# Causal attention with a routed expert layer: joined diagonal key tiles, written-out groups, and side matmuls behind a step's values

## The chip, the cores and the metric

The kernel runs on one core of one Trainium2 chip. The metric is the device time of one execution in microseconds, from the first to the last instruction and what lies around it. Three runs of the kernel before gave 377.74, 378.73 and 380.70 us; the median is 378.73.

## The reference

x has 2048 tokens of 128 features. It is normalised, and two branches are added to it: causal attention with 16 heads of 8 features, and a layer of 8 experts in which each expert takes the 512 tokens with the highest router probability.

```python
xn = _layernorm(x, axis=-1)
# attention, per head
att = jnp.einsum('bhqd,bhkd->bhqk', q, k) * scale
att = jnp.where(causal, att, -jnp.inf)
y = jnp.einsum('bhqk,bhkd->bhqd', softmax(att), v)
# experts
probs = softmax(jnp.einsum('bsd,ed->bse', xn, choice_w))
G, I = jax.lax.top_k(jnp.swapaxes(probs, -1, -2), k)      # k = 512
h = jax.nn.silu(jnp.einsum('bekd,edf->bekf', x_in, w1))    # x_in = xn[I]
x_mlp = jnp.einsum('bekf,efd->bekd', h, w2)
out = x + projected_attention + zeros.at[b_idx, I].add(G[..., None] * x_mlp)
```

## The kernel before, in words

**Tiling.** The heads are done in 4 groups (G) of 4 heads (HG), one group behind the other. In a group the 2048 queries are cut into 4 chunks of 512 (N), and the keys into 16 tiles of 128 (P). A step k is one pair of a query chunk c and a key tile j; causality leaves 4, 8, 12 and 16 steps for the four chunks, 40 in all (NS). The last four steps of a chunk are its diagonal tiles: their key tile lies 0, 128, 256 and 384 queries into the chunk, so they are 512, 384, 256 and 128 queries wide (`off` cuts the rest away) and have one 128 x 128 block that is to be masked.

**A step.** It has two units u = 2k and 2k + 1, one for each pair of heads. For a unit TensorE makes the scores of two heads (`score`, L1146) into one of three double banks of PSUM, ScalarE takes the exponential of both (L691) into `probs`, which has four buffers, one per step. For diagonal steps VectorE masks the block with a minimum (`mask`, L998), once for each unit. Then TensorE multiplies the values with the probabilities of all four heads (`values`, L1163), accumulating over the steps of a chunk in `acc`. The value matmul has float32 operands and is recorded as eight matmuls, 32 output rows for each head. Sums of probabilities come with it, from a column of ones in `v_grp`. At a chunk's end VectorE copies `acc` (L1014), and the next chunk's first values wait for that copy.

**Side work.** Beside the attention steps, groups 0 to 3 do a piece of the router or of an expert in each of some steps, a "turn": group 0 the search for each expert's threshold by bisection (`search`, 30 rounds: TensorE sums comparisons over tokens, L1171; VectorE reduces and makes the next candidate, L890 to L897), group 1 the lists of chosen tokens (`route`, one-hot tiles on VectorE, L941, packed by TensorE, L1196), groups 2 and 3 four experts each (`expert`). An expert has seven turns, one per full-width step: transposing the gathered tokens (L1216), two turns with half of w1 each (L1224), two turns in which only VectorE works (L979), two with half of w2 each (L1232), after which VectorE scales by the gate (`y_exp`, L986) and GpSimd scatters the rows with an added store to DRAM (L600). The hidden halves are copied from PSUM by VectorE (L974), and ScalarE takes their tanh (L680), behind the first exponential of the step two later. All turns share one bank, `spare`.

**Order of the work.** Each engine has its own queue, written by hand and worked through in order; engines meet at semaphores. TensorE's order in step k is: the scores of unit 2k + 3, the turn, the scores of unit 2k + 4, the values of step k. Scores of unit u wait for the exponential of unit u - 3. VectorE's order in groups 0 and 1 is: the copy of `acc` at a chunk's end, the turn of step k, the mask of step k + 1; in groups 2 and 3 the mask comes ahead of the turn. The four lines that matter:

```python
# VectorE, group(): groups 0 and 1 have turn_first=True
if k in turns and turn_first:
    turn(turns.index(k))
if k + 1 < NS:
    mask(g, k + 1)
# TensorE, values(): the first wait of a diagonal step
pe.wait_ge(s_mask, 2 * NT * g + 2 * MASKED.index(k) + 2)
# TensorE, search(): the turn waits for VectorE, and VectorE's next for it
pe.wait_ge(s_above, k)
```

Groups 0 and 1 are written out on TensorE and VectorE, groups 2 and 3 are a loop of two rounds there; ScalarE has two loops of two, and the queue of transfers (SP), which brings the next group's queries and keys, a loop of three and one group written out. The functions that the diff touches:

## Time and profile before

| what | value |
|---|---|
| median of three runs | 378.73 us |
| the profiled execution | 376.79 us |
| its span | 374.7 us |
| around the span | 2.1 us |
| TensorE busy (matmuls) | 326.4 us |
| ScalarE busy | 295.5 us |
| VectorE busy | 218.5 us |
| GpSimd busy | 126.5 us |
| mean granted TensorE clock | 0.954 |

PE is TensorE, PEld its weight loads, DVE VectorE, ACT ScalarE, POOL GpSimd, SP the queue that issues most transfers. Busy times are unions over overlapping instructions, and instructions of one engine can overlap: an exponential of 128 x 1024 is recorded with a duration longer than the distance to the next one's start. From start to start is therefore the measure of a pace, and the duration that of a latency. The group starts can be told by the copies to `v_grp` (L1007, from 51.3 to 280.2 us).

### The profile page before, as it was taken

How to read it: one execution, taken by the hardware profiler on the slowest of the kernel's cores; microseconds unless marked ns; L12 is line 12 of the kernel's file. 1: busy time of each engine (PE TensorE's matmuls, PEld its weight loads, DVE VectorE, ACT ScalarE, POOL GpSimd, SP SyncE). 2: the span in 40 equal slices, each digit the busy share in tenths (PEclk: the TensorE clock that was granted, in tenths of full speed). 3: DMA queues.
4: the chain of work that ended last, by engine and by line, in shares of the span. 5: the costliest groups of instructions: out<-in, count | busy, mean ns of one | idle time of the engine just before them, and what ended most of it. 6: DMA issues, size and time to landing. Idle time of an engine off the chain costs nothing.

```text
span 374.7 us, 7404 instructions
## 1 busy us (share of the span) xinstructions
PE 326.4 (87%) x2453; PEld 109.5 (29%) x2453; DVE 218.5 (58%) x606; ACT 295.5 (79%) x376; POOL 126.5 (34%) x122
## 2 busy tenths in 40 slices
PE   0774848899999699999998989999999899999972
PEld 0442702122222122222222232424242233232362
DVE  4849987866766888669657353342255432526443
ACT  1297729589899688988997989899979899898800
POOL 8420243800000000038830008584868041606150
PEclk9999559699999999999999999999999999999996
DMA  6044575710110210014422113151436131312057
GB/s 169 0 167 117 159 274 209 210 52 0 52 46 22 71 52 24 29 30 132 117 65 71 53 33 52 53 107 52 83 88 128 42 73 14 49 39 21 7 89 224
DMA packets 33679, 30.69 MB, mean 82 GB/s; under 512 B 3688, under 2 KB 28480, under 8 KB 33648
## 3 DMA queue, kind: packets, MB, share of 16 engines
q1 hardware_dynamic: 27248, 24.00, 19.9%
q0 software_dynamic: 6400, 6.30, 10.4%
q8 instruction: 17, 0.28, 0.3%
q14 instruction: 14, 0.11, 0.1%
HBM read 14.36 MB, written 15.93 MB: 81 GB/s over the span
## 4 chain that ended last, share of the span: by engine, by line
PE 69%; DVE 16%; ACT 5%; issue 4%; DMA 4%; POOL 1%; POOLq 1%; DVEq 0%; SPq 0%; ACTq 0%
PE bank L1163 31%; PE bank L1146 20%; PE bank L1232 5%; PE bank L1224 5%; DVE probs L998 4%; ACT probs L691 3%; PE bank L1196 2%; DVE onehot L941 2%; PE bank L1110 2%; DMA x_sb<-in_L_attn_x_dram 1%; DVE cand L895 1%; DMA xn<-total_dram 1%; DMA total_dram<-m_space,token 1%; PE bank L1171 1%; PE bank L1074 1%
## 5 line engine op out<-in xcount | busy, mean ns | idle before, releaser
L691 ACT ACTIVATE probs<-bank 128x1024 f32<-128x1024 f32 (+3 forms) x320 | 264.0, 934 | 41.2 <-PE bank L1146 39.2
L1163 PE MATMUL bank<-probs,v_grp 128*32 128x512 f32 (+3 forms) x1280 | 153.7, 553 | 12.5 <-DVE probs L998 11.8
L1146 PE MATMUL bank<-q_aug,k_aug 51*128 51x512 bf16 (+3 forms) x640 | 106.8, 358 | 3.2 <-ACT probs L691 2.9
L600 POOL DMA_INDIRECT total_dram<-m_space,token x32 | 50.4, 1575 | 93.7 <-DVE m_space L986 86.4
L998 DVE TENSOR_TENSOR probs<-probs,causal 128x256 f32<-128x256 f32 x128 | 50.6, 425 | 37.8 <-ACT probs L691 37.1
L1146 PEld LDWEIGHTS bank<-q_aug,k_aug 51*128 51x128 bf16 x640 | 27.6, 93 | 149.4 <-ACT probs L691 109.7
L941 DVE TENSOR_SCALAR onehot<-slot_iota,slot 128x512 bf16<-128x512 f16 x128 | 37.0, 357 | 9.7 <-PE bank L1196 9.7
L1163 PEld LDWEIGHTS bank<-probs,v_grp 128*32 128x32 f32 x1280 | 25.4, 108 | 51.2 <-DVE probs L998 19.1
L577 POOL DMA_DIRECT2D w_x<-in_L_ffn_w_dram x8 | 7.5, 943 | 90.7 <-DVE gate L960 90.7
L580 POOL DMA_INDIRECT parts<-xn_dram,token x32 | 31.8, 992 | 9.7 <-issue 9.7
L974 DVE COPY m_space<-bank 128x512 f32<-128x512 f32 x16 | 11.0, 687 | 24.2 <-PE bank L1224 24.2
L1232 PE MATMUL bank<-w_x,hT 128*128 128x128 f32 x128 | 18.5, 288 | 2.6 <-DVE hT L979 2.6
L1014 DVE COPY y_acc<-bank 128x512 f32<-128x512 f32 x16 | 11.1, 691 | 14.2 <-PE bank L1163 14.2
L1224 PE MATMUL bank<-xgT,w_x 128*128 128x512 f32 x32 | 18.0, 645 | 0.0
L1232 PEld LDWEIGHTS bank<-w_x,hT 128*128 128x128 f32 x128 | 15.5, 191 | 6.1 <-issue 3.1
L890 DVE TENSOR_REDUCE passed<-bank 128x8 f32<-128x128 f32 x30 | 8.7, 289 | 14.6 <-PE bank L1171 14.6
L1196 PE MATMUL bank<-onehot,parts 128*32 128x512 bf16 x128 | 12.8, 389 | 1.9 <-DVE onehot L941 1.9
L986 DVE TENSOR_TENSOR m_space<-bank,gate 128x512 f32<-128x512 f32 x8 | 5.5, 690 | 13.4 <-PE bank L1232 13.4
L979 DVE SCALAR_TENSOR_TENSOR hT<-th,m_space 128x512 f32<-128x512 f32 x16 | 11.0, 685 | 4.1 <-ACT th L680 4.1
L680 ACT ACTIVATE th<-m_space 128x512 f32<-128x512 f32 x16 | 10.3, 642 | 0.0
L1074 PE MATMUL bank<-xnT,wT 128*128 128x512 f32 x16 | 9.5, 722 | 0.8 <-ACT xnT L617 0.8
L897 DVE TENSOR_TENSOR above<-r_p,cand 128x128 bf16<-128x128 f32 x30 | 8.9, 296 | 1.0
(128 smaller groups left out, 237.7 us busy)
## 6 DMA issues: line engine op xcount, KB each, us to landing
y_dram<-y_acc SPq DMA_DIRECT2D x16, 256.0 KB, 2.2
q_aug<-product_dram SPq DMA_DIRECT2D x32, 96.0 KB
k_aug<-product_dram SPq DMA_DIRECT2D x32, 96.0 KB, 2.4
w_x<-in_L_ffn_w_dram POOLq DMA_DIRECT2D x16, 128.0 KB, 2.8
product_dram<-parts SPq DMA_DIRECT2D x4, 384.0 KB, 3.2
product_dram<-parts SPq DMA_DIRECT2D x6, 256.0 KB, 3.0
product_dram<-parts SPq DMA_DIRECT2D x2, 768.0 KB, 4.8
x_sb<-in_L_attn_x_dram SPq DMA_DIRECT2D x4, 256.0 KB, 4.7
```

The costliest lines, as they stand in the source:

```text
L580: pool.indirect_dma_start(x_got[:, i, t, :], None, xn_dram, bass.IndirectOffsetOnAxis(ap=token[:, e, t:t + 1], axis=0))\
L600: pool.indirect_dma_start(total_dram, bass.IndirectOffsetOnAxis(ap=token[:, e, t:t + 1], axis=0), y_exp[:, e % 2, t, :], None, compute_op= ...
L691: act.activation(probs[:, (u // 2) % PB, 2 * p:2 * p + 2, off:N], scores[u % SB][:, :, off:N], ACT.Exp, scale=SCALE).then_inc(s_exp, 1)
L941: last = dve.tensor_scalar(onehot[:, i % 2, a, :], slot_iota[:, :], slot[:, n, e:e + 1], None, ALU.is_equal)
L998: dve.tensor_tensor(tile, tile, causal[:, :].unsqueeze(1).broadcast_to([P, 2, P]), ALU.min).then_inc(s_mask, 1)
L1014: dve.tensor_copy(y_acc[:, c % 2, :], acc).then_inc(s_accfree, 1)
L1074: pe.matmul(flat(f + i), wT[:, i, :], xnT[:, c * N:(c + 1) * N], start=True, stop=True)
L1146: last = pe.matmul(scores[u % SB][:, a, off:N], k_aug[HEAD_ROWS[a], p, j * P:(j + 1) * P], q_aug[HEAD_ROWS[a], p, c * N + off:(c + 1) * N] ...
L1163: last = pe.matmul(acc[32 * h:32 * h + 32, off:N], v_grp[:, j, h, :], probs[:, k % PB, h, off:N], start=(k in CHUNK_START), stop=(k in CHU ...
L1196: last = pe.matmul(spare[PK_W * a:PK_W * (a + 1), :], payload[:, n, EPP * s + a, :], onehot[:, i % 2, a, :], start=(n == 0), stop=(n == NT ...
L1224: pe.matmul(spare, w1_x[:, i, f * P:(f + 1) * P], xgT[:, :], start=True, stop=True)\
L1232: last = pe.matmul(spare[:, t * C:(t + 1) * C], hT[:, f, t * P:(t + 1) * P], w2_x[:, i, f, :], start=(f == 0), stop=(f == FH - 1))
```

## The change

**Steps and units.** A chunk's four diagonal steps become three. The first is the full-width tile as before. The second holds two tiles, the one of 384 and the one of 128 queries, side by side in the 512 columns of a unit; its mask covers two blocks (the first and the last 128 columns). The third holds the tile of 256 queries and has one unit, for all four heads, 4 x 256 columns. So every unit has 1024 columns; there are 36 steps and 68 units in a group instead of 40 and 80. The third kind of step takes no search turn; experts' turns stand in steps of full width alone, the router's in every step. The banks of PSUM go on turning over from one group to the next, and the first units of a group wait, like all others, for the exponential three units before (the function `before` goes).

**Order on TensorE.** In each step first the scores of the units ahead, together (`scores_ahead`), then the step's values, then the turn.

**Loops.** All groups are written out on all engines, with constants where registers were.

```diff
@@ -47,14 +47,30 @@
     HALF = P // 2
 
 
-    STEPS = [(c, j) for c in range(NC) for j in range(TPC * (c + 1))]
...
+    STEPS = []
+    for _c in range(NC):
+        _d = TPC * _c
+        STEPS += [(_c, [(j, 0, N, 0)], []) for j in range(_d)]
+        STEPS += [(_c, [(_d, 0, N, 0)], [0]),
+                  (_c, [(_d + 1, P, N - P, 0), (_d + 3, N - P, P, N - P)], [0, N - P]),
+                  (_c, [(_d + 2, 2 * P, 2 * P, 0)], [0])]
     NS = len(STEPS)
...
+    HALF_STEP = [k for k in range(NS) if STEPS[k][1][0][2] == N // 2]
+    CHUNK_END = [max(k for k in range(NS) if STEPS[k][0] == c) for c in range(NC)]
...
-    MASKED = [k for k in range(NS) if STEPS[k][1] >= TPC * STEPS[k][0]]
-
-    FIRST_OF_KEYS = [min(k for k in MASKED if STEPS[k][0] == c) for c in range(NC)]
-    NU = 2 * NS
+    FIRST_OF_KEYS = [CHUNK_END[c] - 2 for c in range(NC)]
+
+
+    UNITS = [(k, p) for k in range(NS) for p in ([(0, 1)] if k in HALF_STEP else [(0,), (1,)])]
+    NU = len(UNITS)
+    FIRST_UNIT = [min(u for u in range(NU) if UNITS[u][0] == k) for k in range(NS)]
+    LAST_UNIT = [max(u for u in range(NU) if UNITS[u][0] == k) for k in range(NS)]
+
+    MASKS = [sum(len(UNITS[u:v]) for u, v in
+                 [(FIRST_UNIT[i], LAST_UNIT[i] + 1) for i in range(k + 1) if STEPS[i][2]]) for k in range(NS)]
     SB = 3
...
-    SEARCH_STEPS = [k for k in range(NS) if WIDTH[k] > N // 2]
-    EXPERT_STEPS = [k for k in range(NS) if WIDTH[k] == N]
-    ROUTE_STEPS = [k for k in range(NS) if WIDTH[k] > P]
+    SEARCH_STEPS = [k for k in range(NS) if k not in HALF_STEP]
+    EXPERT_STEPS = [k for k in range(NS) if k not in HALF_STEP and k + 1 not in HALF_STEP]
+    ROUTE_STEPS = list(range(NS))
...
-            with sp.Fori(0, G - 1) as g:
-                group(g, False)
-            group(G - 1, True)
+            for g in range(G):
+                group(g, g == G - 1)
...
+            def expert_tanh(g, i):
                 if i % TPE in H_TURN:
-                    e, f = EPG * x + i // TPE, H_TURN.index(i % TPE)
...
+            def exponentials(g, u):
+                k, pairs = UNITS[u]
+                buf = scores[(NU * g + u) % SB]
+                own = probs[:, (NS * g + k) % PB]
+                act.wait_ge(s_sready, NU * g + u + 1)
+                if u == FIRST_UNIT[k]:
+
+                    act.wait_ge(s_pfree, NS * g + k + 1)
+                if k in HALF_STEP:
+                    src = buf[:, :, :].rearrange("q a (p n) -> q a p n", p=2)
+                    dst = own[:, :, 0:N // 2].rearrange("q (p a) n -> q a p n", a=2)
+                else:
+                    src, dst = buf[:, :, :], own[:, 2 * pairs[0]:2 * pairs[0] + 2, :]
+                act.activation(dst, src, ACT.Exp, scale=SCALE).then_inc(s_exp, 1)
+
+            for g in range(G):
                 for u in range(NU):
-                    c, j = STEPS[u // 2]
-                    off = max(0, j - TPC * c) * P
-                    p = u % 2
-                    act.wait_ge(s_sready, NU * g + u + 1)
-                    if p == 0:
-
-                        act.wait_ge(s_pfree, NS * g + u // 2 + 1)
-                    act.activation(probs[:, (u // 2) % PB, 2 * p:2 * p + 2, off:N],
-                                   scores[u % SB][:, :, off:N], ACT.Exp, scale=SCALE).then_inc(s_exp, 1)
-                    if extra and p == 0 and u // 2 - 2 in EXPERT_STEPS:
-                        extra(EXPERT_STEPS.index(u // 2 - 2))
-
-            with act.Fori(0, EXPERT_G) as g:
-                group(g)
-            with act.Fori(0, G - EXPERT_G) as x:
-
-                group(x + EXPERT_G, lambda i: expert_tanh(x, i))
+                    exponentials(g, u)
+                    k = UNITS[u][0]
+                    if g >= EXPERT_G and u == FIRST_UNIT[k] and k - 2 in EXPERT_STEPS:
+                        expert_tanh(g, EXPERT_STEPS.index(k - 2))
 
...
             def mask(g, k):
-                c, j = STEPS[k]
-                if k in MASKED:
-                    off = (j - TPC * c) * P
-                    for p in range(2):
-
-                        dve.wait_ge(s_exp, NU * g + SB + 2 * k + p + 1)
-                        tile = probs[:, k % PB, 2 * p:2 * p + 2, off:off + P]
-                        dve.tensor_tensor(tile, tile, causal[:, :].unsqueeze(1).broadcast_to([P, 2, P]),
-                                          ALU.min).then_inc(s_mask, 1)
+                places = STEPS[k][2]
+                if not places:
+                    return
+                own = probs[:, (NS * g + k) % PB].rearrange("q h (b n) -> q h b n", n=P)
+                own = own[:, :, 0:TPC:TPC - 1, :] if len(places) == 2 else own[:, :, 0:1, :]
+                for u in range(FIRST_UNIT[k], LAST_UNIT[k] + 1):
+                    pairs = UNITS[u][1]
+                    tile = own[:, 2 * pairs[0]:2 * pairs[-1] + 2]
+                    dve.wait_ge(s_exp, NU * g + SB + u + 1)
+                    dve.tensor_tensor(tile, tile, causal[:, :].unsqueeze(1).unsqueeze(1).broadcast_to(
+                        [P, 2 * len(pairs), len(places), P]), ALU.min).then_inc(s_mask, 1)
...
-                for k, (c, j) in enumerate(STEPS):
+                for k in range(NS):
+                    c = STEPS[k][0]
                     if k in CHUNK_END:
 
...
             group(THRESHOLD_G, SEARCH_STEPS, search, turn_first=True)
             group(ROUTE_G, ROUTE_STEPS, route, turn_first=True)
-            with dve.Fori(0, G - EXPERT_G) as x:
-                group(x + EXPERT_G, EXPERT_STEPS, lambda i: expert(x, i))
+            for g in range(EXPERT_G, G):
+                group(g, EXPERT_STEPS, lambda i: expert(g - EXPERT_G, i))
 
...
             def score(g, u):
-                k, p = u // 2, u % 2
-                c, j = STEPS[k]
-                off = max(0, j - TPC * c) * P
-                if p == 0 and k in CHUNK_START:
+                k, pairs = UNITS[u]
+                c, blocks, _ = STEPS[k]
+                if u == FIRST_UNIT[k] and k in CHUNK_START:
                     pe.wait_ge(s_stage_q[c], 16 * 4 * (g + 1))
-                if p == 0 and k in FIRST_OF_KEYS:
+                if u == FIRST_UNIT[k] and k in FIRST_OF_KEYS:
                     pe.wait_ge(s_stage_k[c], 16 * 2 * (g + 1))
 
-                pe.wait_ge(s_exp, NU * g + SB + before(u))
-                for a in range(2):
-                    last = pe.matmul(scores[u % SB][:, a, off:N],
-                                     k_aug[HEAD_ROWS[a], p, j * P:(j + 1) * P],
-                                     q_aug[HEAD_ROWS[a], p, c * N + off:(c + 1) * N], start=True, stop=True)
+                pe.wait_ge(s_exp, NU * g + u + 1)
+                for i, p in enumerate(pairs):
+                    for j, first, width, at in blocks:
+                        at += i * (N // 2)
+                        for a in range(2):
+                            last = pe.matmul(scores[(NU * g + u) % SB][:, a, at:at + width],
+                                             k_aug[HEAD_ROWS[a], p, j * P:(j + 1) * P],
+                                             q_aug[HEAD_ROWS[a], p, c * N + first:c * N + first + width],
+                                             start=True, stop=True)
                 last.then_inc(s_sready, 1)
 
             def values(g, k):
-                c, j = STEPS[k]
-                off = max(0, j - TPC * c) * P
+                c, blocks, places = STEPS[k]
                 if k == 0:
                     pe.wait_ge(s_vgrp, g + 1)
                 if k in CHUNK_START:
                     pe.wait_ge(s_accfree, NC * g + c + 1)
-                if k in MASKED:
-                    pe.wait_ge(s_mask, 2 * NT * g + 2 * MASKED.index(k) + 2)
+                if places:
+                    pe.wait_ge(s_mask, MASKS[-1] * g + MASKS[k])
                 else:
-                    pe.wait_ge(s_exp, NU * g + SB + 2 * k + 2)
-                for h in range(HG):
-                    last = pe.matmul(acc[32 * h:32 * h + 32, off:N], v_grp[:, j, h, :], probs[:, k % PB, h, off:N],
-                                     start=(k in CHUNK_START), stop=(k in CHUNK_END))
+                    pe.wait_ge(s_exp, NU * g + SB + LAST_UNIT[k] + 1)
+                for j, first, width, at in blocks:
+                    for h in range(HG):
+                        last = pe.matmul(acc[32 * h:32 * h + 32, first:first + width], v_grp[:, j, h, :],
+                                         probs[:, (NS * g + k) % PB, h, at:at + width],
+                                         start=(k in CHUNK_START), stop=(k in CHUNK_END))
                 last.then_inc(s_pfree, 1)
...
+            def scores_ahead(g, k):
+
+                for u in range(FIRST_UNIT[k] + LEAD, LAST_UNIT[k] + LEAD + 1):
+                    if u < NU:
+                        score(g, u)
+                    elif g + 1 < G:
+                        score(g + 1, u - NU)
+
             def group(g, turns, turn):
                 for k in range(NS):
-                    if 2 * k + LEAD < NU:
-                        score(g, 2 * k + LEAD)
+                    scores_ahead(g, k)
+                    values(g, k)
                     if k in turns:
                         turn(turns.index(k))
-                    if 2 * k + LEAD + 1 < NU:
-                        score(g, 2 * k + LEAD + 1)
-                    if k == NS - 1:
-                        next_group(g)
-                    values(g, k)
-
-            def next_group(g):
-
-                if isinstance(g, int):
-                    for u in range(LEAD):
-                        score(g + 1, u)
-                else:
-                    with pe.If(g < G - 1):
-                        for u in range(LEAD):
-                            score(g + 1, u)
 
             for u in range(LEAD):
                 score(0, u)
             group(THRESHOLD_G, SEARCH_STEPS, search)
             group(ROUTE_G, ROUTE_STEPS, route)
-            with pe.Fori(0, G - EXPERT_G) as x:
-                group(x + EXPERT_G, EXPERT_STEPS, lambda i: expert(x, i))
+            for g in range(EXPERT_G, G):
+                group(g, EXPERT_STEPS, lambda i: expert(g - EXPERT_G, i))
 
...
```

On TensorE, first group, from the last unmasked step of chunk 2 into its diagonal (bank: PSUM; q_aug, k_aug: scores; v_grp: values; above: the search's comparisons). Before:

```order
L1163 MATMUL bank<-probs,v_grp 32x512 [waits probs_ready]
L1163 MATMUL bank<-probs,v_grp 32x512 x3
L1146 MATMUL bank<-q_aug,k_aug 128x384 [waits probs_ready]
L1146 MATMUL bank<-q_aug,k_aug 128x384
L1171 MATMUL bank<-above,ones_pp 128x128 [waits candidates_compared]
L1146 MATMUL bank<-q_aug,k_aug 128x256 [waits probs_ready]
L1146 MATMUL bank<-q_aug,k_aug 128x256
L1163 MATMUL bank<-probs,v_grp 32x512 [waits causal_masked]
L1163 MATMUL bank<-probs,v_grp 32x512 x3
```

After:

```order
L1178 MATMUL bank<-probs,v_grp 32x512 [waits probs_ready]
L1178 MATMUL bank<-probs,v_grp 32x512 x3
L1187 MATMUL bank<-above,ones_pp 128x128 [waits candidates_compared]
L1160 MATMUL bank<-q_aug,k_aug 128x384 [waits probs_ready]
L1160 MATMUL bank<-q_aug,k_aug 128x384
L1160 MATMUL bank<-q_aug,k_aug 128x128 x2
L1160 MATMUL bank<-q_aug,k_aug 128x256 [waits probs_ready]
L1160 MATMUL bank<-q_aug,k_aug 128x256 x3
L1178 MATMUL bank<-probs,v_grp 32x512 [waits causal_masked]
L1178 MATMUL bank<-probs,v_grp 32x512 x3
L1187 MATMUL bank<-above,ones_pp 128x128 [waits candidates_compared]
```

The search's matmul of the masked step stood two places ahead of that step's values (the L1171 in the middle) and now stands behind them; the two units' scores stand together.

On VectorE, same place: passed, cand, thr and above are the search's turn, probs the mask, y_acc the copy of the sum. Before, from the chunk's last turn:

```order
L890 TENSOR_REDUCE passed<-bank 128x8 [waits tokens_above_counted]
L891 SCALAR_TENSOR_TENSOR cand<-passed,cand 128x8 [waits threshold_step]
L893 TENSOR_TENSOR thr<-thr,cand 128x8 [waits threshold_step]
L895 TENSOR_SCALAR cand<-thr 128x8 [waits threshold_step]
L897 TENSOR_TENSOR above<-r_p,cand 128x128 [waits threshold_step]
L998 TENSOR_TENSOR probs<-probs,causal 128x2x128 [waits probs_ready] x4
L1014 COPY y_acc<-bank 128x512 [waits y_sent1,probs_used]
```

After:

```order
L900 TENSOR_REDUCE passed<-bank 128x8 [waits tokens_above_counted]
L901 SCALAR_TENSOR_TENSOR cand<-passed,cand 128x8 [waits threshold_step]
L903 TENSOR_TENSOR thr<-thr,cand 128x8 [waits threshold_step]
L905 TENSOR_SCALAR cand<-thr 128x8 [waits threshold_step]
L907 TENSOR_TENSOR above<-r_p,cand 128x128 [waits threshold_step]
L1010 TENSOR_TENSOR probs<-probs,causal 128x4x128 [waits probs_ready]
L1027 COPY y_acc<-bank 128x512 [waits y_sent1,probs_used]
```

Turn and mask keep their order; four masks of two blocks are now one of four.

On TensorE, third group, a step of the first expert with half of w1 (xgT, w_x). Before:

```order
L1146 MATMUL bank<-q_aug,k_aug 128x512 [waits probs_ready]
L1146 MATMUL bank<-q_aug,k_aug 128x512
L1223 ISA
L1224 MATMUL bank<-xgT,w_x 128x512 [waits hidden_copied]
L1144 REGISTER_ALU
L1146 MATMUL bank<-q_aug,k_aug 128x512 [waits probs_ready]
L1146 MATMUL bank<-q_aug,k_aug 128x512
L1163 MATMUL bank<-probs,v_grp 32x512 [waits probs_ready]
L1163 MATMUL bank<-probs,v_grp 32x512 x3
```

After:

```order
L1160 MATMUL bank<-q_aug,k_aug 128x512 [waits probs_ready]
L1160 MATMUL bank<-q_aug,k_aug 128x512
L1160 MATMUL bank<-q_aug,k_aug 128x512 [waits probs_ready]
L1160 MATMUL bank<-q_aug,k_aug 128x512
L1178 MATMUL bank<-probs,v_grp 32x512 [waits probs_ready]
L1178 MATMUL bank<-probs,v_grp 32x512 x3
L1240 MATMUL bank<-xgT,w_x 128x512 [waits hidden_copied]
```

The w1 matmul has moved from between the two units' scores to behind the step's values.

## Rows read from the trace of the kernel before

**Rows 1.** Page, part 1: busy us (share of the span) and instructions.
```profile
PE 326.4 (87%) x2453; PEld 109.5 (29%) x2453; DVE 218.5 (58%) x606; ACT 295.5 (79%) x376; POOL 126.5 (34%) x122
```

**Rows 2.** Busy time by stretch (us; PE, PEld, DVE, ACT, POOL, granted clock, DMA, GB/s).
```profile
67.10:73.90 6.80, 6.43 (x34) 1.03 (x26) 5.91 (x17) 2.91 (x5) 6.21 (x10) 0.50 0.85 252
...
203.40:281.40 78.00, 75.83 (x576) 24.54 (x576) 31.55 (x61) 69.78 (x89) 38.78 (x33) 1.00 0.31 67
```

**Rows 3.** Timeline, first group, full step (start, us, engine, line, out<-in, count).
```profile
81.60 1.06 PE L1163 MATMUL bank<-probs,v_grp 128*32 128x512 f32 x8
...
82.60 0.39 PE L1146 MATMUL bank<-q_aug,k_aug 51*128 51x512 bf16 x2
...
82.92 0.23 PE L1171 MATMUL bank<-above,ones_pp 128*128 128x128 bf16 x1
...
83.44 1.06 PE L1163 MATMUL bank<-probs,v_grp 128*32 128x512 f32 x8
```

**Rows 4.** Timeline, ScalarE, same stretch.
```profile
79.27 10.21 ACT L691 ACTIVATE probs<-bank 128x1024 f32<-128x1024 f32 x11
```

**Rows 5.** Groups by shape: busy us, mean ns | idle before, releaser.
```profile
L691 ACT ACTIVATE probs<-bank 128x1024 f32<-128x1024 f32 x224 | 212.2, 1068 | 11.8 <-PE bank L1146 11.2
...
L998 DVE TENSOR_TENSOR probs<-probs,causal 128x256 f32<-128x256 f32 x128 | 50.6, 425 | 37.8 <-ACT probs L691 37.1
...
L691 ACT ACTIVATE probs<-bank 128x256 f32<-128x256 f32 x32 | 12.2, 382 | 8.3 <-PE bank L1146 7.5
...
L680 ACT ACTIVATE th<-m_space 128x512 f32<-128x512 f32 x16 | 10.3, 642 | 0.0
...
L986 DVE TENSOR_TENSOR m_space<-bank,gate 128x512 f32<-128x512 f32 x8 | 5.5, 690 | 13.4 <-PE bank L1232 13.4
```

**Rows 6.** Timeline, first group, into the diagonal of chunk 3.
```profile
118.50 0.23 PE L1171 MATMUL bank<-above,ones_pp 128*128 128x128 bf16 x1
...
118.77 0.29 DVE L890 TENSOR_REDUCE passed<-bank 128x8 f32<-128x128 f32 x1 [0.70 <-PE bank L1171]
...
119.91 0.93 DVE L998 TENSOR_TENSOR probs<-probs,causal 128x256 f32<-128x256 f32 x2
...
120.89 0.64 PE L1163 MATMUL bank<-probs,v_grp 128*32 128x512 f32 x4 [0.17 <-DVE probs L998]
```

**Rows 7.** Timeline, TensorE, first group, diagonal of chunk 2.
```profile
90.78 1.06 PE L1163 MATMUL bank<-probs,v_grp 128*32 128x512 f32 x8
...
97.46 0.42 PE L1163 MATMUL bank<-probs,v_grp 128*32 128x128 f32 x8
...
98.75 0.64 PE L1163 MATMUL bank<-probs,v_grp 128*32 128x512 f32 x4
```

**Rows 8.** Timeline, third group, expert steps.
```profile
261.74 1.06 PE L1163 MATMUL bank<-probs,v_grp 128*32 128x512 f32 x8
...
263.06 1.13 PE L1224 MATMUL bank<-xgT,w_x 128*128 128x512 f32 x2
...
264.22 0.69 DVE L974 COPY m_space<-bank 128x512 f32<-128x512 f32 x1 [2.00 <-PE bank L1224]
...
264.44 1.06 PE L1163 MATMUL bank<-probs,v_grp 128*32 128x512 f32 x8
...
268.67 1.07 PE L1163 MATMUL bank<-probs,v_grp 128*32 128x512 f32 x8
...
270.20 1.06 PE L1163 MATMUL bank<-probs,v_grp 128*32 128x512 f32 x8
```

**Rows 9.** Waits: engine, line <- releaser: us in total, times, longest us.
```profile
PE bank L1232 <- DVE hT L979: 2.6, 2, 1.3
```

**Rows 10.** Timeline, fourth group, last diagonal.
```profile
352.19 1.16 PE L1232 MATMUL bank<-w_x,hT 128*128 128x128 f32 x8
...
353.50 1.06 PE L1163 MATMUL bank<-probs,v_grp 128*32 128x512 f32 x8
353.50 0.69 DVE L986 TENSOR_TENSOR m_space<-bank,gate 128x512 f32<-128x512 f32 x1
```

25 lines of the change are left out of this document (9 added, 16 removed).

## Prediction

> **What bounds the kernel now.** I read the page first, then the busy time by stretch, then the timeline step by step. TensorE is busy for 87% of the span and ScalarE for 79% [rows 1], an average over four head groups that do different side work. By stretch: the third group, which carries experts, has TensorE busy 75.83 of 78.00 us and ScalarE 69.78 [rows 2]. So in the expert groups nearly every microsecond that TensorE is given or spared counts, and ScalarE has some 8 us of air in a group.
>
> I call V(k) the eight value matmuls of step k, S a unit's scores, T(k) the side matmul of a step (search, router, expert). In the first group the V at 81.60 is followed by S 82.60, T 82.92, another S, and V 83.44: 1.84 us a step [rows 3]. Its pieces, from start to start, are V 1.00, S 0.32, T 0.20, S 0.32: TensorE works without a break. ScalarE's exponentials in that stretch, eleven in 10.21 us, the last one about 1.07 long by the group's mean, start (10.21 - 1.07) / 10 = 0.91 us apart [rows 4, 5]: 1.82 a step. The two engines are almost level there, and neither can catch up quickly.
>
> **The diagonal units.** Exponential instructions go from 320 (224 of 1024 elements and three shorter forms of 32 each) to 272, 48 fewer, masks from 128 [rows 5] to 80, most of them of twice the size. TensorE's columns are the same (384 + 128 instead of two steps, 256 for four heads instead of two units), so where TensorE is the bound the packing gives only a few tile switches. An exponential of 1024 elements takes 1.07 and one of 256 takes 0.38 [rows 5]: 0.69 for 768 elements, 0.92 per 1024, which leaves 0.15 fixed in an instruction, but the start spacing of 0.91 shows that most of that overlaps with the next one. I value the 48 instructions at nothing on the path and hide them behind TensorE; the ends are -2.4 us (48 x 0.05, were ScalarE the bound) and 0. The Trainium skill, "ScalarE: Activation LUTs", section "What ACT_TABLE_LOAD costs", gives an activation 186 ns plus 0.833 ns per element; by it 48 fewer would spare 8.9 us and the sum would come out 8.9 lower. The rows agree with that as the length of one, not as the distance of two.
>
> **What the new order does in the first group.** The order on VectorE does not change: turn(k) of the search (L890 to L897) waits for T(k), and mask(k+1) stands behind it. Before, T(k) stands ahead of V(k), so that chain runs beside a whole V. The last diagonal shows how tight that is: T at 118.50, reduce 118.77, above 119.69, masks 119.91 for 0.93, V at 120.89 [rows 6], 2.39 us from T to the V of the next step, of which TensorE already idles 0.17. After, T(k) stands behind V(k). Then V(k+1) <- mask(k+1) <- turn(k) <- T(k) <- V(k) is one serial loop, at each masked step. Its links: V 1.00, then 2.39 from T to V. For the joined step b each mask has 512 elements, which costs 0.69 as the other VectorE operation of that size on 128 partitions does [rows 5] against 0.42, so 2 x 0.27 = 0.54 more: 2.93. For the half step c one such mask: 2.39 - 0.93 + 0.69 = 2.15, with waits say 2.3. V takes 1.06 for 512 columns [rows 3] and 0.42 for 128 [rows 7], so 0.21 for each 128, and start to start 0.15 more: V of b, in two pieces, is 1.14, V of c 0.57. From the short last V to the next chunk's V it is 1.29 now (97.46 to 98.75 [rows 7]: the accumulator's copy), so 1.50 with 0.21 more columns. A chunk's end, from V(a-1) to the next chunk's first V, is then (1.00 + 2.39) + (1.00 + 2.93) + (1.14 + 2.3) + 1.50 = 12.3 us. Now it is 98.75 - 90.78 = 7.97 [rows 7]. That is +4.3 for three loops, 1.43 each. Chunk 0 has one loop (the first turn needs no matmul), chunks 1 and 2 have three, chunk 3 two (behind the joined step the search marks its result and waits for no T): nine loops, 12.9 us. The 21 full steps gain from one S beside the other (two in a row take 0.54, not 0.64: a step without T is 1.53 [rows 8], less 1.00 for V) until ScalarE's 1.82 stops them: -0.5. **First group +12.4.** ScalarE's lead of three units does not absorb this: it keeps ScalarE busy, but V is late, and afterwards TensorE needs 1.73 and ScalarE 1.82 a step, so nothing is made good.
>
> **TensorE's clock.** The granted clock was 0.50 (1.2 GHz) for the 6.80 us from 67.10 [rows 2], at the diagonal of chunk 1, where the search waits for VectorE already. The new diagonals leave TensorE idle about half the time. Not falling again costs 0; 1.2 GHz through the diagonals of chunks 2 and 3 and a step or two behind each costs up to 7 (seven or eight V at up to 1.0 each). I take one more fall as long as the one shown, two V: +2.0. The Trainium skill, "TensorE: Matmul & The Clock Gate", section "HAM oscillation — how this bites in real kernels", warns of just such a kernel that waits between bursts; by it the sum would be nearer +7.
>
> **Router group.** Its T of 512 bf16 columns is taken like an S, 0.32; the step is then 0.32 + 0.32 + 0.32 + 1.00 = 1.96 now, 1.86 after, about 24 times: -2.4. The turn makes one-hots for the next T, so there is no loop in ordinary masked steps; two joined masks are a little cheaper than three or four, -0.5 in all. Four turns do need their own step's T and have a mask or a copy behind them (ranks, the first list, the last copy, the last list); each comes a V later: +4.0. **+1.1**, ends -2.9 and +5.
>
> **Expert groups.** A step with T is 264.44 - 261.74 = 2.70 now [rows 8], 2.60 after; one without is 270.20 - 268.67 = 1.53 in both. 20 steps with T in a group: -2.0. One stall goes: TensorE waits 2 x 1.3 us for hT (L979) [rows 9], at the diagonal of chunk 1; after, V covers it: -1.3. A new one comes: ScalarE runs tanh for step k behind the first exponential of step k+2. That exponential's scores now come before V(k) and T(k), not behind T(k). Now T at 263.06 leads to the copy at 264.22 (0.69) [rows 8], 1.16 later, and none of the 16 tanh waited [rows 5]. After, with V(k) at 0: T 1.00, copy 2.16 to 2.85, while the exponential started at about 0.9 and ScalarE is free at 1.8: tanh waits 1.1 us, and the next one 0.3 more. Followed on, the next exponentials start at 3.4 and 4.3, the second tanh at 5.5, the exponential behind it at 6.0, done at 7.0. TensorE, with V at 0, 2.60, 5.20 and 6.74, asks for that one at 6.5, before the V of the second step without T, and gets it at 7.1; there the pair of S is split as well, so V comes at 7.4, 0.7 late, and a step on another 0.25 late: 0.95 in all. Four experts in a group: +3.8. Four accumulator waits with the wider last V: +0.8. **+1.3 in the third group, +1.1 up to the last diagonal of the fourth.** Ends: -3.3 without any tanh effect, +4.
>
> **The end.** The last expert's product (T at 352.19, y_exp at 353.50 [rows 10]) starts POOL's scatters, which lead to the end. It now stands ahead of the diagonal's V (353.50); behind it, it ends 1.00 + 1.16 later instead of level: **+2.2**. The written-out loops change no order inside a group. No row prices a loop's turn by itself; TensorE's idle time in the looped third group, 78.00 - 75.83 = 2.2 us [rows 2], bounds the gain, and as much the loss from more code to load. I put it at 0, since that idle time has other causes named above.
>
> **Sum.** 12.4 + 2.0 + 1.1 + 1.3 + 1.1 + 2.2 = 20.1 us on the profiled execution's 376.8: 396.9, say 397. That execution is 1.9 below the median of 378.7 and within the runs' 3.0 spread, so I add nothing.
>
> **Rivals.**
> A, faster: the loop through VectorE never decides, since exponentials and tile switches carry the time. Place: diagonals of the first group. Price: the chunk's end shrinks to TensorE's own work of about 6.7 instead of 7.97, -3.9 in three chunks; with -0.5, -2.9, twice -3.3, and the end's +2.2 it is 365 us. It decides if T to V takes less than the 0.73 that T and two S give as cover; 2.39 speaks against it. 0.08.
> B, expert groups gain: tanh finds its operand because TensorE's lead over ScalarE is smaller than I assume. Then twice the 3.8 go, 397 - 7.6 = 389.4, and with a third off the first group's term 385. For it: ScalarE is now idle in steps with T. 0.20.
> C, the clock stays at half in the first group's diagonals and on into full steps, and the router's late turns meet it: +5 to +8, 402 to 405. 0.17.
> D, halfway: the loop costs half of 12.4 and the expert groups gain as in A, 397 - 6.2 - 7.6 - 2.0 (no fall of the clock) = 381, near the edge of no change. 0.05.
> The forecast: 0.50.
>
> **How the numbers follow.** About 1% is what a measurement of this kernel can tell from no change. Faster 0.08 is A; the same 0.05 is D; slower 0.87 is the forecast with B and C. The range runs from B's low end to just past C's: 385 to 406, with A and D outside and a little above.
>
> **What would show it.** In the profile after, the first group's V starts at the diagonals should be about 3.4, 3.9 and 3.4 us apart and VectorE's reduce should come 0.27 behind a T that follows V; the expert groups should last 79 us with tanh rows that sat idle behind VectorE's copy; y_exp of the last expert should start 2 us after the last 512-wide masked V. I am wrong if chunk 2 of the first group ends in under 9 us, if tanh shows no wait, or if exponentials start under 0.91 apart in full steps.

## The result, and the profile after

Slower, as forecast. Five runs of the changed kernel have a median of 396.06 us (393.26 to 396.56), five of the kernel before in the same session 379.82: a ratio of 1.043, 95% interval 1.038 to 1.047. The forecast was 397. The profiled execution took 393.26 with a span of 391.5, 16.8 more than before; both profiled executions are at the fast end of their kernel's runs, 2.8 and 3.0 under these medians.

The page after: busy time, the slices of TensorE and the granted clock.

```profile
PE 320.4 (82%) x2453; PEld 107.8 (28%) x2453; DVE 214.9 (55%) x558; ACT 290.1 (74%) x328; POOL 128.1 (33%) x122
...
PE   1775856589599749997997899999998999999971
...
PEclk9997558969779998998999999999999999999995
```

TensorE is busy for 6 us less and the span is 17 us longer [rows 1]: the loss is waiting. Each digit is a fortieth of the span, 9.8 us: the low ones in the 6th to the 14th (first group) and a few in the 15th to the 22nd (router) show where. The groups' starts, read from the first V of each:

| stretch | before | after | difference | forecast |
|---|---|---|---|---|
| up to the first V | 52.6 | 53.5 | +0.9 | 0 |
| first group (search) | 75.8 | 88.1 | +12.3 | +12.4 and +2.0 of clock |
| second group (router) | 75.0 | 76.3 | +1.2 | +1.1 |
| third group (experts) | 78.1 | 78.8 | +0.7 | +1.3 |
| fourth, to its last diagonal | 72.1 | 72.5 | +0.4 | +1.1 |
| end | 21.2 | 22.4 | +1.2 | +2.2 |

Every group's time holds the luck of the clock as well. In the first group TensorE's granted clock was at half for 11.1 us before and for 25.3 after (over the group it is 0.93 and 0.86). The kernel of e6 below has the first group's order of the kernel before, but its clock was at half there for 22.3 us, and the group took 80.4 instead of 75.8. That is 0.42 us for each further microsecond at half clock. Other pairs of profiles with one order give 0.17 (e10 against the changed kernel, first group: 89.4 against 88.1, 32.8 at half against 25.3) and 0.45 (e1 against it, third group: 80.1 against 78.8, 2.9 against 0). So a difference of a microsecond between two single profiles shows nothing before the clock has been compared.

The waits after, in total, times and longest (us). The first row was 11.8, 15 times, before; the second 14.6, 23 times; the third had no counterpart.

```profile
PE bank L1178 <- DVE probs L1010: 33.6, 20, 5.4
DVE passed L900 <- PE bank L1187: 29.5, 30, 3.4
ACT th L688 <- DVE m_space L984: 8.9, 8, 1.5
```

The timeline after, first group, diagonal of chunk 2 (L1178: V, L1187: T, L1160: S, L900 to L907: the search's turn, L1010: masks, L1027: copy of acc). It answers to [rows 6, 7].

```profile
96.02 1.06 PE L1178 MATMUL bank<-probs,v_grp 128*32 128x512 f32 x8
...
97.01 0.23 PE L1187 MATMUL bank<-above,ones_pp 128*128 128x128 bf16 x1
...
97.28 0.29 DVE L900 TENSOR_REDUCE passed<-bank 128x8 f32<-128x128 f32 x1 [0.52 <-PE bank L1187]
...
98.42 0.76 DVE L1010 TENSOR_TENSOR probs<-probs,causal 128x256 f32<-128x256 f32 x2
...
99.23 1.06 PE L1178 MATMUL bank<-probs,v_grp 128*32 128x512 f32 x8 [1.31 <-DVE probs L1010]
...
100.23 0.23 PE L1187 MATMUL bank<-above,ones_pp 128*128 128x128 bf16 x1
...
102.98 1.93 PE L1178 MATMUL bank<-probs,v_grp 128*32 128x384 f32 x16 [1.98 <-DVE probs L1010]
...
104.85 0.29 PE L1187 MATMUL bank<-above,ones_pp 128*128 128x128 bf16 x1
...
107.05 1.08 PE L1178 MATMUL bank<-probs,v_grp 128*32 128x256 f32 x8 [1.38 <-DVE probs L1010]
...
109.03 1.93 PE L1178 MATMUL bank<-probs,v_grp 128*32 128x512 f32 x8
```

Here the loop can be read link by link: V 96.02, T 97.01, reduce 97.28, masks 98.42, V 99.23, and again. The V are 3.21, 3.75, 4.07 and 1.98 apart, 13.0 us where it was 7.97 before; forecast 12.3. In the full steps ahead of that diagonal, on the other hand, TensorE runs at 1.70 a step:

```profile
89.08 1.07 PE L1178 MATMUL bank<-probs,v_grp 128*32 128x512 f32 x8
...
90.78 1.06 PE L1178 MATMUL bank<-probs,v_grp 128*32 128x512 f32 x8
```

The timeline after, third group, the first expert's two steps with w1 (L1240) and the two free steps behind them; it answers to [rows 8].

```profile
225.32 1.07 PE L1178 MATMUL bank<-probs,v_grp 128*32 128x512 f32 x8
225.62 0.63 ACT L688 ACTIVATE th<-m_space 128x512 f32<-128x512 f32 x1 [1.08 <-DVE m_space L984]
...
226.32 1.12 PE L1240 MATMUL bank<-xgT,w_x 128*128 128x512 f32 x2
...
227.91 1.07 PE L1178 MATMUL bank<-probs,v_grp 128*32 128x512 f32 x8
...
230.13 1.07 PE L1178 MATMUL bank<-probs,v_grp 128*32 128x512 f32 x8
...
232.09 1.07 PE L1178 MATMUL bank<-probs,v_grp 128*32 128x512 f32 x8
```

The step with T takes 2.59, as forecast, the first tanh idles 1.08 (forecast 1.1), and the two free steps take 2.22 and 1.96 where they were 1.53 each.

### The profile page after: what moved, and what is told of

Its sections match the earlier page's. It is cut to its first block, busy times and chain, and to the rows that moved or that the text cites. A ratio compares the mean times of both kernels' runs of the same rounds, so it can differ in the third digit from the quotient of the medians.

```text
span 391.5 us, 6404 instructions
## 1 busy us (share of the span) xinstructions
PE 320.4 (82%) x2453; PEld 107.8 (28%) x2453; DVE 214.9 (55%) x558; ACT 290.1 (74%) x328; POOL 128.1 (33%) x122
## 4 chain that ended last, share of the span: by engine, by line
PE 59%; DVE 22%; ACT 9%; issue 5%; DMA 3%; POOL 1%; POOLq 0%; SPq 0%; DVEq 0%; ACTq 0%
PE bank L1178 30%; PE bank L1160 12%; ACT probs L703 6%; DVE probs L1010 5%; PE bank L1248 4%; PE bank L1240 4%; DVE y_acc L1027 2%; PE bank L1122 2%; PE bank L1212 1%; DVE m_space L984 1%; PE bank L1187 1%; DVE onehot L951 1%; PE bank L1232 1%; DMA xn<-total_dram 1%; DVE cand L905 1%
## 5 line engine op out<-in xcount | busy, mean ns | idle before, releaser
L703 ACT ACTIVATE probs<-bank 128x1024 f32<-128x1024 f32 x272 | 256.4, 1060 | 50.8 <-PE bank L1160 49.9
L1178 PE MATMUL bank<-probs,v_grp 128*32 128x512 f32 (+3 forms) x1280 | 155.4, 569 | 36.0 <-DVE probs L1010 33.6
L1160 PE MATMUL bank<-q_aug,k_aug 51*128 51x512 bf16 (+3 forms) x640 | 92.8, 366 | 6.1 <-ACT probs L703 5.5
L608 POOL DMA_INDIRECT total_dram<-m_space,token x32 | 51.4, 1606 | 95.8 <-DVE m_space L996 88.5
L1010 DVE TENSOR_TENSOR probs<-probs,causal 128x512 f32<-128x512 f32 (+1 forms) x80 | 44.8, 580 | 26.5 <-ACT probs L703 26.2
L1178 PEld LDWEIGHTS bank<-probs,v_grp 128*32 128x32 f32 x1280 | 28.0, 112 | 96.9 <-issue 39.2
L1160 PEld LDWEIGHTS bank<-q_aug,k_aug 51*128 51x128 bf16 x640 | 22.2, 95 | 76.1 <-ACT probs L703 50.8
L951 DVE TENSOR_SCALAR onehot<-slot_iota,slot 128x512 bf16<-128x512 f16 x128 | 37.8, 362 | 7.3 <-PE bank L1212 7.0
L900 DVE TENSOR_REDUCE passed<-bank 128x8 f32<-128x128 f32 x30 | 8.7, 292 | 29.5 <-PE bank L1187 29.5
L1027 DVE COPY y_acc<-bank 128x512 f32<-128x512 f32 x16 | 11.1, 692 | 19.0 <-PE bank L1178 19.0
L1240 PE MATMUL bank<-xgT,w_x 128*128 128x512 f32 x32 | 18.0, 645 | 0.0
L1187 PEld LDWEIGHTS bank<-above,ones_pp 128*128 128x128 bf16 x30 | 2.9, 97 | 28.4 <-DVE above L907 18.8
```

Source lines behind the costliest of these rows:

```text
L608: pool.indirect_dma_start(total_dram, bass.IndirectOffsetOnAxis(ap=token[:, e, t:t + 1], axis=0), y_exp[:, e % 2, t, :], None, compute_op= ...
L703: act.activation(dst, src, ACT.Exp, scale=SCALE).then_inc(s_exp, 1)
L951: last = dve.tensor_scalar(onehot[:, i % 2, a, :], slot_iota[:, :], slot[:, n, e:e + 1], None, ALU.is_equal)
L1010: dve.tensor_tensor(tile, tile, causal[:, :].unsqueeze(1).unsqueeze(1).broadcast_to([P, 2 * len(pairs), len(places), P]), ALU.min).then_in ...
L1027: dve.tensor_copy(y_acc[:, c % 2, :], acc).then_inc(s_accfree, 1)
L1160: last = pe.matmul(scores[(NU * g + u) % SB][:, a, at:at + width], k_aug[HEAD_ROWS[a], p, j * P:(j + 1) * P], q_aug[HEAD_ROWS[a], p, c * N ...
```

## The experiments

All but e4 and e6 start from the changed kernel; e4 and e6 start from the one before. Each was timed in three rounds beside the kernel before (medians 378.8 to 379.9). All compute the whole reference. The code is cut to the lines that matter. "g1 72.5" means that the first group took 72.5 us in the profiled execution.

### e1_search_early: the old order, in the first group alone

```diff
- scores_ahead(g, k)
+ early = g == THRESHOLD_G
+ scores_ahead(g, k, slice(0, 1))
+ if early and k in turns:
+     turn(turns.index(k))
+ scores_ahead(g, k, slice(1, None))
  values(g, k)
- if k in turns:
+ if not early and k in turns:
      turn(turns.index(k))
```

The slice picks which of the step's units get their scores.

> The changed kernel, with TensorE's order of the kernel before (scores, turn, scores, values) in the first group alone. Theory L (a serial loop values, search matmul, VectorE's turn, mask, next values): the first group falls from 88 us to between 73 and 76, the diagonal of its chunk 2 from 13.0 us to under 8, the granted clock there stays 1.00, and the profiled execution comes to about 380 (393 less 13). Rival P (the joined and half steps with their larger masks cost it, the order is harmless): no change, 391 to 395. Rival U (the written-out loops cost it): no change.

Measured: 378.36 us, ratio 1.000 (0.997 to 1.003); g1 72.5, g2 76.1, g3 80.1. The profile of e1 at the same diagonal:

```profile
90.14 1.06 PE L1178 MATMUL bank<-probs,v_grp 128*32 128x512 f32 x8
...
91.46 0.23 PE L1187 MATMUL bank<-above,ones_pp 128*128 128x128 bf16 x1
...
91.94 1.07 PE L1178 MATMUL bank<-probs,v_grp 128*32 128x512 f32 x8
...
94.21 1.07 PE L1178 MATMUL bank<-probs,v_grp 128*32 128x384 f32 x16 [0.40 <-DVE probs L1010]
...
95.95 0.64 PE L1178 MATMUL bank<-probs,v_grp 128*32 128x256 f32 x8 [0.34 <-DVE probs L1010]
...
97.41 1.06 PE L1178 MATMUL bank<-probs,v_grp 128*32 128x512 f32 x8
```

V to V this chunk's end takes 7.27 instead of 13.0: T stands ahead of V, so the search's turn runs beside it. The place of one small matmul in one group is worth 17.7 us in the medians (396.06 - 378.36) and 15.0 in the profiled spans, about as much as the whole change costs (16.2 and 16.8). That sum holds the clock too: in the first group it was at half for 11.6 us here and for 25.3 in the changed kernel.

### e2_masks_first: TensorE untouched, masks ahead of the turn on VectorE

```diff
- group(THRESHOLD_G, SEARCH_STEPS, search, turn_first=True)
+ group(THRESHOLD_G, SEARCH_STEPS, search)
```

> The changed kernel, with the mask of step k+1 ahead of the search's turn k on VectorE in the first group, as groups 3 and 4 have it. TensorE's order is untouched, so the search matmul still stands behind the values. L: the mask no longer waits for that matmul, the loop is open, and the first group falls to 74 to 77 us, the whole to about 381. P and U: no change, 391 to 395. Were it the place on TensorE as such (its matmul late, whoever waits), also no change.

Measured: 379.62, ratio 1.000 (0.998 to 1.002); g1 74.5. Here TensorE's order is that of the changed kernel, word for word, and the loss is gone all the same. So what costs is the loop V, T, turn, mask, V, and it can be cut at either of the two edges tried. TensorE's order by itself costs the first group little: g1 is 2.0 above e1's 72.5 and 1.3 below the 75.8 of the kernel before.

### e3_tanh_late: tanh behind the step's second exponential

```diff
- if g >= EXPERT_G and u == FIRST_UNIT[k] and k - 2 in EXPERT_STEPS:
+ if g >= EXPERT_G and u == LAST_UNIT[k] and k - 2 in EXPERT_STEPS:
```

> The changed kernel, with ScalarE's tanh for step k behind the second exponential of step k+2, not the first. L: the 8 waits of tanh (8.9 us in all) go, the gap between the V of the two steps without a side matmul falls from 2.21 and 1.92 to about 1.6 and 1.8, and the two expert groups lose 2 to 4 us each: 386 to 389. Rival: the waits lie in ScalarE's slack and nothing moves, 392 to 394.

Measured: 391.2, ratio 1.032 (1.028 to 1.037), less gain than expected; in the profile the third group takes 77.2 against 78.8, 0.4 per expert, not 0.95, and from the fourth group's start to the end it is 92.9 against 94.9, 0.5 per expert. No tanh waits any more, but ScalarE's wait for scores in the third group grows. The waits of ScalarE in that group, of the changed kernel (217.8 to 296.6 us):

```profile
ACT probs L703 <- PE bank L1160: 5.5, 10, 1.6
ACT th L688 <- DVE m_space L984: 4.3, 4, 1.1
```

of e3 (218.8 to 296.0):

```profile
ACT probs L703 <- PE bank L1160: 8.3, 15, 1.6
```

and of e11_best_orders below (196.1 to 272.3), with the old order in the expert groups:

```profile
ACT probs L703 <- PE bank L1160: 7.0, 19, 1.0
```

The timeline of e3, TensorE, the same expert's free steps:

```profile
228.95 1.07 PE L1178 MATMUL bank<-probs,v_grp 128*32 128x512 f32 x8
...
230.49 1.06 PE L1178 MATMUL bank<-probs,v_grp 128*32 128x512 f32 x8
...
232.27 0.39 PE L1160 MATMUL bank<-q_aug,k_aug 51*128 51x256 bf16 x4 [0.39 <-ACT probs L703]
...
232.73 1.06 PE L1178 MATMUL bank<-probs,v_grp 128*32 128x512 f32 x8
```

The first free step has shrunk from 2.22 to 1.54, but the second has grown from 1.96 to 2.24, with TensorE waiting for an exponential. 4.3 us of waits for tanh's operand are gone and 2.8 of waits for scores have come. ScalarE waits 9.8, 8.3 and 7.0 us in the group in these three kernels, and the group takes 78.8, 77.2 and 76.2. But its work is the same in all three, so time less waits has to come out equal (69.0, 68.9, 69.2) and doesn't say which engine sets the pace; TensorE is idle 4.8, 3.9 and 1.7 us there. What the rows show is that the new order leaves ScalarE longer without scores even when no tanh waits, and TensorE waiting for the exponential that comes late. e11 differs from e3 both in T's place and in the split pair of S; no run parts the two.

### e4_order_alone: the kernel before, with T behind V and both S first

```diff
- if k in turns:
-     turn(turns.index(k))
  if 2 * k + LEAD + 1 < NU:
      score(g, 2 * k + LEAD + 1)
...
  values(g, k)
+ if k in turns:
+     turn(turns.index(k))
```

> The kernel before with one edit: on TensorE both scores of a step, its values and then the turn. Diagonals stay four steps, loops stay loops. L: the first group grows from 76 to about 87 (nine or more loops of 1.4 us or less, since its masks are shorter), tanh waits appear in the expert groups, and the whole comes to 388 to 394. P or U: 375 to 379.

Measured: 409.27, ratio 1.079 (1.074 to 1.084), far above what was expected; g1 90.2, g2 82.8, g3 83.2, against 75.8, 75.0 and 78.1. The order costs 30 us where the diagonals are not packed. What the expectation left out is at least in part the clock: from the first group's first V to the fall at the end it was at half for 65.4 us, in the kernel before for 11.1 and in the changed kernel for 32.1.

### e5_pack_alone: packed diagonals, the old order in all groups

As e1, with `early = True`.

> The changed kernel with the old order on TensorE in all groups (scores, turn, scores, values): what is left of the change is the joined diagonals and the written-out loops. L: the tanh waits go, the first group is 73 us as in the run with the early search, the router group 74 to 77, the expert groups 76 to 78; 371 to 377. P: the joined steps cost, 380 or more.

Measured: 373.98, ratio 0.987 (0.980 to 0.993); g1 74.0, g2 78.2, g3 76.2, and 91.3 from the fourth group's start to the end (94.9 in the changed kernel, 93.2 before). Packing, with the loops written out, makes the kernel faster, by 5.1 us by the ratio of the runs and 2.0 in the profiled executions. There the router group alone is slower (78.2 against 75.0, with the clock at half for 3.4 us of it against none). In the expert groups the old order is better than the new one, 76.2 against e3's 77.2 and the changed kernel's 78.8.

### e6_loops_alone: the kernel before, with the loops written out

```diff
- with pe.Fori(0, G - EXPERT_G) as x:
+ for x in range(G - EXPERT_G):
```

The same was done on ScalarE, VectorE and SP.

> The kernel before with its loops over groups written out on all engines and nothing else. L: no change, 377 to 380 as the median. U: 385 or more, or below 374 if turning a loop costs something.

Measured: 379.78, ratio 1.000 (0.995 to 1.004). The 0 of the forecast holds to within 2 us. The profiled execution has g1 80.4, g2 75.0, g3 78.0: the first group is the one whose clock was at half for 22.3 us.

### e7_masks_first: masks ahead of turns in the first and the router group

```diff
- group(THRESHOLD_G, SEARCH_STEPS, search, turn_first=True)
- group(ROUTE_G, ROUTE_STEPS, route, turn_first=True)
+ group(THRESHOLD_G, SEARCH_STEPS, search)
+ group(ROUTE_G, ROUTE_STEPS, route)
```

> The changed kernel with masks ahead of turns on VectorE in the first and the router group. L: as the run with masks first in the first group alone, and the four late turns of the router group (ranks, lists, last copy) lose the V and the masks behind them: that group from 76 to 70 to 73 us, the whole 373 to 376. Rival: the router's turns are held by the one-hots, which now come later, and the group grows.

Measured: 370.84, ratio 0.980 (0.975 to 0.985), below the 373 expected; g1 72.8, g2 69.5, g3 78.8. Two arguments removed from the changed kernel take it from 4% slower to 2% faster. The router's 6.7 us (76.3 - 69.5) come in the main from its late turns, and some from the clock, at half for 6.8 us in the changed kernel's group and 3.4 here. In the changed kernel, the rank turn at the second group's start:

```profile
141.57 1.07 PE L1178 MATMUL bank<-probs,v_grp 128*32 128x512 f32 x8 [1.36 <-DVE probs L1010]
...
142.70 0.28 PE L1198 MATMUL bank<-sel_sum,ones_pp 128*128 128x272 bf16 x1
...
143.01 0.17 DVE L931 COPY sel_count<-bank 128x8 f32<-128x8 f32 x1 [1.59 <-PE bank L1198]
...
144.52 1.14 DVE L951 TENSOR_SCALAR onehot<-slot_iota,slot 128x512 bf16<-128x512 f16 x4
145.57 1.29 DVE L1010 TENSOR_TENSOR probs<-probs,causal 128x512 f32<-128x512 f32 x2
...
146.92 1.87 PE L1178 MATMUL bank<-probs,v_grp 128*32 128x384 f32 x16 [3.40 <-DVE probs L1010]
```

The masks stand behind the ranks and four one-hots, and V comes 5.35 us after the V before it. In the kernel before the masks stood behind the same one-hots, and V came 3.14 us after V (128.34 to 131.48):

```profile
129.62 1.14 DVE L941 TENSOR_SCALAR onehot<-slot_iota,slot 128x512 bf16<-128x512 f16 x4
130.67 0.76 DVE L998 TENSOR_TENSOR probs<-probs,causal 128x256 f32<-128x256 f32 x2
```

### e8_combined: e7, e3, and the last expert's last T ahead of V

> The changed kernel with masks ahead of turns everywhere, tanh behind the second exponential, and in the last group the last expert's second w2 turn ahead of the values of its step. L: the gains add up: 3 to 4 us under the run with masks first in both groups, plus 1 to 2 at the end, 368 to 371, faster than both kernels. Rival: the scatters that lead to the end are not what ends last, then 370 to 373.

Measured: 367.46, ratio 0.971 (0.966 to 0.976), just below the 368 to 371 expected; g3 77.2, and 92.6 to the end against 94.8 in e7's profile. The two edits added to e7 bring 3.4 us together.

### e10_end_early: only the last T ahead of its V

```diff
+ early = g == G - 1 and k == NS - 3
  scores_ahead(g, k)
+ if early and k in turns:
+     turn(turns.index(k))
  values(g, k)
- if k in turns:
+ if not early and k in turns:
      turn(turns.index(k))
```

> The changed kernel with one turn moved: only the last expert's second half of w2 (the last turn of the fourth group) stands ahead of its step's values again, everything else is as in the changed kernel. Theory (the end's term): y_exp starts with the last full-width masked values instead of 2.2 us behind them, so what follows starts earlier: the end, from those values to the last instruction, goes from 22.4 back to about 21.2 us, 1.2 us less, and the time is about 394.8 against 396.1. The prediction's own figure would give 2.2 less, 393.9. Rival: the end hangs on the last chunk's own values and division, then nothing changes (396).

Measured: 393.52 (393.22 to 394.94), ratio 1.037 (1.031 to 1.044). The interval overlaps that of the changed kernel, so the times alone don't tell the two apart. In the profiles, from the full-width V ahead of the last diagonal to the end it is 391.99 - 367.52 = 24.5 us against 391.53 - 366.45 = 25.1. With the changed kernel's order the same stretch is 24.6 us in e1, 24.7 in e2 and 24.9 in e7. So the move is worth 0.1 to 0.6, hardly more than such stretches differ by themselves, since the diagonal's own V comes later by T:

```profile
367.52 1.07 PE L1178 MATMUL bank<-probs,v_grp 128*32 128x512 f32 x8
...
370.14 1.16 PE L1248 MATMUL bank<-w_x,hT 128*128 128x128 f32 x8
...
371.23 2.45 PE L1178 MATMUL bank<-probs,v_grp 128*32 128x512 f32 x32
...
371.70 0.69 DVE L996 TENSOR_TENSOR m_space<-bank,gate 128x512 f32<-128x512 f32 x1
```

### e11_best_orders: e7's first half, e5's expert groups

The edit of e7, and e1's loop with another condition:

```diff
+ early = g >= EXPERT_G
```

> The changed kernel with masks ahead of turns on VectorE in the first two groups (as in e7_masks_first, TensorE's order there as in the changed kernel) and, in the two expert groups, the order of the kernel before on TensorE: scores, turn, scores, values, with tanh where it was. Theory: the groups add up, since nothing is carried across a group's start. First and second group as in e7_masks_first (72.8 and 69.5 us), third and fourth as in e5_pack_alone (76.2, and 91.3 to the end): 53.7 + 72.8 + 69.5 + 76.2 + 91.3 = 363.5 of span, a time of about 365, 4 below the 370.8 of e7_masks_first with its 78.8 and 94.7. Rival: the expert groups are bound by TensorE's sum of work and take the same in any order once tanh does not wait, then it comes out as e8_combined did (367.5).

Measured: 364.88 (364.53 to 365.23), ratio 0.961 (0.956 to 0.966), g1 74.6, g2 68.8, g3 76.2, and 91.1 to the end; span 363.3 where 363.5 was expected. This is the fastest version, 3.9% below the kernel before and 7.9% below the changed one. The groups' times add up, each to within 2 us (g1 is 1.8 over e7's, what lies ahead of it 1.0 and g2 0.7 under).

## Why the prediction was right, point by point

**The loop in the first group: the mechanism right, the size in part by luck.** The group lost 12.3. That isn't the 12.4 alone: the clock's 2.0 was to fall there too, which makes 14.4. At the four chunks' ends, from the last unmasked V (in chunk 0 the first V) to the next chunk's first V, it lost 1.3, 1.2, 5.0 and 2.0, together 9.6 where nine loops of 1.43 were to cost 12.9. At chunk 1 the forecast was far over: that end took 11.1 us before already, with the clock at half for 6.8 of them [rows 2], and 12.3 after, +1.2 for a forecast of +4.3. The full steps lost 2.7, where -0.5 and the clock's 2.0 were forecast.

In chunk 2, 5.0 us for a forecast of 4.3, the links were a little shorter than forecast: T to the next V took 2.22, 2.75 and 2.20 (97.01 to 99.23, 100.23 to 102.98, 104.85 to 107.05) against 2.39, 2.93 and 2.3. What made the diagonal 13.0 rather than 12.3 is the clock: from the V at 102.98 to its T it took 1.87 where the forecast had 1.14 (at full clock such a V takes 1.00, 219.96 to 220.96 in the third group), and from the V at 107.05 to the next 1.98 where it had 1.50, together 1.21. At full clock, in chunk 3, two loops cost 2.0 us where 2.9 were forecast. e1 and e2 cut the loop at two different edges and both bring the whole kernel back to 1.000, so it is shown that the loop is the cause; how the 12.3 divide between its waits and the clock that fell with them is not.

**"Nothing is made good": that step failed.** The prediction let the full steps gain "until ScalarE's 1.82 stops them". But ScalarE has done the three units ahead while V was late, and TensorE runs at 1.70 a step and eats that lead at 0.11 a step. In chunk 3 the lead is used up after four such steps, and only then does ScalarE's pace hold, as forecast:

```profile
120.95 1.07 PE L1178 MATMUL bank<-probs,v_grp 128*32 128x512 f32 x8
...
122.79 1.07 PE L1178 MATMUL bank<-probs,v_grp 128*32 128x512 f32 x8
```

So part of the loss is made good. This stayed small beside the 12 us, and the clock took it back.

**TensorE's clock: the sort right, the count wrong, the 2.0 us too few.** One fall more was forecast, for 2.0 us. In the stretch between the first group's start and the end, it fell once before and five times after, in the router group too. Busy time and instructions by stretch, after (PE, PEld, DVE, ACT, POOL, then granted clock, DMA share, GB/s):

```profile
61.70:65.10 3.40, 3.29 (x17) 0.64 (x21) 1.05 (x5) 2.15 (x3) 1.91 (x1) 0.50 0.24 68
78.80:85.60 6.80, 5.39 (x27) 0.77 (x25) 3.02 (x11) 3.16 (x4) 0.00 (x0) 0.50 0.11 41
102.70:112.90 10.20, 8.54 (x48) 1.77 (x52) 3.69 (x13) 4.16 (x6) 0.00 (x0) 0.50 0.07 26
147.00:150.50 3.50, 3.50 (x30) 1.17 (x34) 1.52 (x5) 0.70 (x1) 0.00 (x0) 0.51 0.00 0
181.20:184.60 3.40, 3.40 (x24) 0.54 (x18) 3.40 (x10) 1.49 (x2) 2.50 (x3) 0.50 0.33 95
```

In the fall at 102.7 the three V that can be compared lost 0.79, 0.48 and about 0.9 (1.93 for 1.06). TensorE waits in two of the five stretches (1.4 of 6.8 us and 1.7 of 10.2) and hardly in the others. All told the clock was at half for 21.0 us more than before up to the fall at the end (32.1 against 11.1). At the 0.17 to 0.45 us for each such microsecond of the section on the result, this is 4 to 9 us, an estimate, and not 2.0. The Trainium skill, "TensorE: Matmul & The Clock Gate", section "HAM oscillation — how this bites in real kernels", was right as a warning that a kernel which waits between bursts loses clock. The +7 that the prediction read out of it lies inside that estimate and is neither shown nor excluded; no run took the clock apart. So the total came near the forecast with the clock undervalued and the loops overvalued.

**Router group: the sum right (+1.2 for +1.1), by larger terms than forecast.** The full steps gained more (1.75 after, 1.97 before, forecast 1.86), and the late turns cost more. The rank turn's V to V went from 3.14 to 5.35, +2.2 where the forecast had +1.0. Of these, 1.67 is that the ranks begin 1.44 behind V (143.01 - 141.57) instead of 0.23 ahead of it (128.11 against 128.34), and 0.53 that the two masks take 1.29 instead of 0.76. e7 shows the size: with the masks first, the same order on TensorE takes 69.5, 5.5 less than before.

**Expert groups: sign right, cause half right.** Forecast +1.3 and +1.1, measured +0.7 and +0.4. The steps with T took the forecast 2.59, the first tanh idled 1.08, the second hardly, the stall on hT went, and the two free steps lost 4.18 - 3.06 = 1.1 per expert (forecast 0.95). But the prediction laid all of it on tanh ("ends: -3.3 without any tanh effect"), and e3, in which no tanh waits, gets back only 0.4 to 0.5 of an expert's 0.95. What is left goes with ScalarE waiting longer for scores, against the 8 us of air that the forecast gave it; that this is its cause is argued from e3's rows and not tried by itself. Rival B, which gave back all 3.8 when tanh didn't wait, would have failed for the same reason. (In rival D the expert groups "gain as in A", but its sum takes B's 7.6; A's -3.3 in place of +1.3 and +1.1 is 9.0, and D would be 380, not 381.) And the -2.0 that the paired scores save in steps with T is more than lost: e11 has 2.69 there, and its third group still takes 2.6 less.

**The end: right mechanism, half the size.** y_exp came 371.27 - 369.08 = 2.19 after the diagonal's V, as forecast, but the end moved by 1.2. The failed step is that the prediction took V as a fixed mark: where T stands ahead of V, V is late itself. e10 gives 0.1 to 0.6 for the move.

**Packing: valued at 0, worth 2 to 5 us.** e5 against the kernel before is -2.0 in the profiled spans and -5.1 by the ratio (the interval reaches from -2.5 to -7.7); the end of the forecast's range was -2.4. "I value the 48 instructions at nothing" is the step that failed: the third group and what follows the fourth's start both took 1.9 less. In the third group ScalarE's busy time fell by 1.0 (69.8 to 68.8) and TensorE's by 1.4 (75.9 to 74.5); through which of them the gain came is open. The Trainium skill's 8.9 us, from "ScalarE: Activation LUTs", section "What ACT_TABLE_LOAD costs", did not show: ScalarE's busy time fell by 1.7 in e5 and by 295.5 - 290.1 = 5.4 in the changed kernel. The same passage also says that back-to-back activations overlap by about 93 ns, which the prediction left out; with it 48 fewer would spare 48 x 0.093 = 4.5 us of ScalarE's time, an estimate from that page's figures. The order, then, cost 18.8 us by the spans (391.5 - 372.7) and 22.1 by the medians: the total of 16.2 came out near the forecast with a gain that was left out and an order that cost about the 20 allowed. That too is partly luck.

**Under the new order packing is worth more**: 409.27 - 396.06 = 13.2 us. How the 30 us of e4 divide was not taken apart. The clock was at half for 54.3 us more than before (65.4 against 11.1), by the same estimate 9 to 24 of them; in the changed kernel it was 21.0 more. TensorE's waits for masks are 31.7 us in it against 11.8 before, and tanh waits for its operand there too:

```profile
PE bank L1163 <- DVE probs L998: 31.7, 28, 5.5
...
ACT th L680 <- DVE m_space L974: 6.9, 9, 1.1
```
